# Attention matmuls of both halves together, and both softmax halves first on VectorE, in the first and third cross attention

## What is computed

```python
# A0
Q = q @ Wq.T + bq; K = k @ Wk.T + bk; V = k @ Wv.T + bv
scores = einsum('bhqd,bhkd->bhqk', Q_, K_) / D_HEAD ** 0.5
scores = where(causal, scores, -1e9)
att = einsum('bhqk,bhkd->bhqd', softmax(scores), V_)
att_h = layer_norm(att + q)
# A2
scores = einsum('bqhd,bkhd->bhqk', q, k)
scores = where(mask == 0, -1e20, scores)
out = einsum('bhqk,bkhd->bqhd', softmax(scores / sqrt(EMBED)), v)
x = layernorm(out @ w_out + b_out + query)
```

## Time and profile before

| | us |
|---|---|
| median of three executions | 2589.75 |
| the profiled execution | 2593.18 |
| its span, first to last instruction | 2591.4 |
| A0, first to last score product | 14.9 to 412 |
| A2, first to last score product | 1029 to 1404 |

### The profile page before, as it was taken

One profiled execution on the slowest core, in us unless ns is written; L12 is line 12 of the kernel. 1 busy time (PEld: TensorE's weight loads), 2 busy tenths in 40 slices (PEclk: granted clock), 3 DMA queues, 4 the chain that ended last, 5 costly groups with the idle time before them and its releaser, 6 DMA issues. The chain is left out here.

```text
span 2591.4 us, 83416 instructions
## 1 busy us (share of the span) xinstructions
PE 2355.9 (91%) x26926; PEld 1806.6 (70%) x26926; DVE 1894.2 (73%) x4003; ACT 1498.3 (58%) x3407; POOL 1539.6 (59%) x2438
## 2 busy tenths in 40 slices
PE   6999998987777777999998988999999999999899
PEld 4666666975656565777776876777777777777587
DVE  4676764139999994677776667888888888888566
ACT  4777775558888884777776542444444444444333
POOL 2555555127888884455556776666666666666332
PEclk9999999989999997999999998999999999999999
DMA  4111111235555551222121223333333333333111
GB/s 121 38 38 39 36 40 44 71 109 153 148 155 148 154 153 39 51 46 46 47 47 41 65 63 83 92 94 97 97 95 95 94 94 96 94 94 93 50 58 54
DMA packets 443043, 211.78 MB, mean 82 GB/s; under 512 B 206400, under 2 KB 433856, under 8 KB 442816
## 3 DMA queue, kind: packets, MB, share of 16 engines
q1 hardware_dynamic: 442944, 210.51, 30.7%
HBM read 113.36 MB, written 29.88 MB: 55 GB/s over the span
## 5 line engine op out<-in xcount | busy, mean ns | idle before, releaser
L666 PE MATMUL bank<-sb_ident,sb_region 128*77 128x128 f32 x3072 | 413.8, 278 | 85.7 <-ACT sb_pT L754 84.8
L666 PEld LDWEIGHTS bank<-sb_ident,sb_region 128*77 128x77 f32 x3072 | 350.2, 151 | 139.9 <-issue 137.7
L754 ACT ACTIVATE sb_pT<-bank 77x1024 f32<-77x1024 f32 x384 | 391.6, 1020 | 67.1 <-PE bank L666 67.0
L858 DVE TENSOR_REDUCE sb_max<-bank 128x8 f32<-128x616 f32 x256 | 203.5, 795 | 205.8 <-PE bank L648 118.0
L1528 ACT ACTIVATE sb_l<-sb_l 128x640 f32<-128x640 f32 x128 | 94.5, 738 | 386.2 <-DVE sb_l L1576 386.2
L749 ACT ACTIVATE sb_region<-sb_region 128x616 f32<-128x616 f32 x384 | 276.8, 721 | 1.4 <-POOL sb_region L995 1.4
L1649 POOL TENSOR_TENSOR sb_pn<-sb_l,sb_r_all 128x512 f32<-128x512 f32 x128 | 134.7, 1052 | 233.4 <-DVE sb_r_all L1586 229.5
L1398 PE MATMUL bank<-sb_region,sb_wqkv 128*128 128x128 f32 x2048 | 255.2, 279 | 1.6 <-DVE sb_region L1564 0.8
L682 PE MATMUL bank<-sb_pT,sb_v 77*32 77x128 f32 x6144 | 248.2, 279 | 3.6 <-ACT sb_pT L754 3.2
L1438 PE MATMUL bank<-sb_wvo,sb_region 128*64 128x512 f32 x1024 | 248.0, 605 | 0.0
L1398 PEld LDWEIGHTS bank<-sb_region,sb_wqkv 128*128 128x128 f32 x2048 | 243.6, 195 | 4.1 <-DVE sb_region L1564 1.5
(11 more groups left out here) (183 smaller groups left out, 5645.4 us busy)
## 6 DMA issues: line engine op xcount, KB each, us to landing
sb_region<-in_side SPq DMA_DIRECT2D x64, 616.0 KB, 3.8
sb_pT<-sb_region SPq DMA_DIRECT2D x512, 64.0 KB, 2.1
sb_kF<-sb_region SPq DMA_DIRECT2D x512, 64.0 KB, 2.1
scratch_after_A<-sb_y SPq DMA_DIRECT2D x256, 64.0 KB, 1.8
sb_fx<-scratch_after_A SPq DMA_DIRECT2D x96, 128.0 KB, 2.1
sb_mask<-in_mask SPq DMA_DIRECT2D x64, 154.0 KB, 2.2
sb_x<-scratch_after_F SPq DMA_DIRECT2D x128, 64.0 KB, 1.9
sb_ctx<-in_ctxT SPq DMA_DIRECT2D x192, 38.5 KB, 1.9
```

The lines of the kernel that those rows point to most:

```text
L666: mm = nc.tensor.transpose(two[0:C, h * T:(h + 1) * T], p_s[b.par][:, head * C:(head + 1) * C], ident[:])
L754: nc.scalar.activation(pT_s[k][:], two[0:C, :], ACT.Copy).then_inc(pT_kept.sem(b), 1)
L858: nc.vector.tensor_reduce(dst, by_bank_and_head(scores_half(k)), AX.X, ALU.max).then_inc(max_made.sem(b), 1)
```

## The change

In A0 and A2, TensorE's `attend(b, 0)` is taken from the end of step b and done in step b + 1, straight before `attend(b, 1)`, behind `scores(b + 2)`. On VectorE, `peak` and `shift` of the second half follow those of the first at once; `invert`, `normalise` and `sums` come after both. `sum_context(b+1)` moves to the end of the step, and the statistics are taken at the end of a step (of b - 2) and no longer at the start of the next one (of b - 3), which is the same batch. No operation is added or taken away, and A1 keeps its order.

```diff
--- before.py
+++ after.py
@@ -598,6 +598,7 @@
             w = cross[ph]
             prev = phase_before(ph)
             taken = s_weighted if ph == "A1" else shifted
+            together = ph != "A1"
 
             def out_banks_left(b):
 
@@ -708,6 +709,8 @@
                 if has(1):
                     scores(b + 1)
                 if has(-1):
+                    if together:
+                        attend(b + -1, 0)
                     attend(b + -1, 1)
                 if has(-2) and ph != "A0":
                     transpose_o(b + -2, has(1))
@@ -737,7 +740,7 @@
                     transpose_x(b + 3)
                 if has(2) and ph == "A0":
                     mask_early(b + 2, b + 1 if has(1) else None)
-                if has(0):
+                if has(0) and not together:
                     attend(b, 0)
             drive(pe, NB, step, reach=REACH)
 
@@ -959,26 +962,25 @@
                     aggregate(b + -2)
 
             def step(b, has):
-                if has(1) and ph == "A0":
-                    sum_context(b + 1)
-                if has(-3):
-                    statistics(b + -3)
                 if has(1):
                     peak(b + 1, 0)
                 if has(-3):
                     aggregate(b + -3)
                 if has(1):
                     shift(b + 1, 0)
+                    peak(b + 1, 1)
+                    shift(b + 1, 1)
                 if has(-1):
                     invert(b + -1)
                     normalise(b + -1)
                 if has(-2):
                     sums(b + -2)
-                if has(1):
-                    peak(b + 1, 1)
-                    shift(b + 1, 1)
+                if has(1) and ph == "A0":
+                    sum_context(b + 1)
                 if has(2) and ph == "A2":
                     key_bias(b + 2)
+                if has(-2):
+                    statistics(b + -2)
             drive(dve, NB, step_weighted if ph == "A1" else step, reach=REACH)
 
         def cross_gpsimd(pool, ph):
```

## The result

The changed kernel takes 2629.97 us (median of four executions, 2629.05 to 2633.8) against 2590.8 us before (2586.35 to 2592.21). The ratio is 1.0153, with a 95% interval of 1.0138 to 1.0167: 39 us slower, where 42 had been forecast. The profiled execution took 2630.25 us, its span 2628.5.

A forecast was written before the change was run, and what follows sets the result against it. TensorE's in-order queue, with scores waiting for the query copy, was taken as the bound. Over 64 steps each, A0 +16.6 us and A2 +25.6 us, together 42.2 on 2589.8, gave 2632 us; range 2606 to 2656.

The forecast's parts named there:

- The bound: A0 and A2: TensorE's in-order queue plus small stalls sets the period, TensorE busy 92 to 94%; scores need the query copy.
- The attention block at its new place: Between scores and attention of half 1: paid in full, adding 0.45 us a step (0.33 to 0.58).
- The saving at its old place: End of step: mostly covered by the query copy wait; saves 0.14 us in A0, nothing in A2.
- An ordinary step: Saving and added block summed: +0.31 us in A0, +0.45 us in A2.
- The loop's end: Jump of TensorE's four-step loop, 0.21 us in A0, 0.20 in A2: hidden afterwards, -0.05 us a step.
- The steps written out at the ends of the phases: Steps outside the hardware loop in A0 and A2: counted like the others, within 64 steps a phase.
- the clock: Granted clock in A0 and A1: at its upper level, 1.00, so left out of the sum.
- The spare time of the normalisation: VectorE's delayed normalisation before the query projection: 0.3 us to spare in A0, so no cost.
- rival C: VectorE becomes late: each 0.1 us beyond the spare 0.3 costs 6.4 us a phase; 2645 us, chance 0.10.
- The stall of the keys: Keys wait 0.17 us for VectorE's first shift in A0: goes away, but not on the path.
- rival B: The keys' stall was on the path: A0 gains 0.17 to 0.2 us a step more; 2620 us, chance 0.08.
- Rival A: Mode changes decide, query wait doesn't hold TensorE: -0.13 us a step in A0, -0.24 in A2; 2566 us, chance 0.09.

The follow-up runs named there:

- e7: The changed kernel with the attention of half 0 computed a second time, unused, at its old place at the end of the step: 2639.65 us, ratio 1.0199.
- e3: The kernel before with only TensorE's new order, VectorE keeping its old step: 2630.06 us, ratio 1.0156.
- e5: The kernel before with query projection and transpose of x moved ahead of the transposes of half 1 in A0 and A2: 2556.4 us, ratio 0.9872.
- e4: The changed kernel with TensorE's order put back, so only VectorE's order is new: 2612.0 us, ratio 1.0090.
- e9: e6 with VectorE's order changed to peak 0, shift 0, peak 1, invert, normalise, shift 1, sums: 2532.35 us, ratio 0.9778.
- e6: e5 plus the paired attention and ScalarE's query and x copies ahead of the first exponential, VectorE's order old: 2577.5 us, ratio 0.9949.

## Why the prediction was right, point by point

**The bound.** That TensorE's chain through the query copy sets the period held: filling its shadow (e7) cost nothing in A2 and 0.14 us in an ordinary step of A0, as the release 0.13 earlier lets expect, and VectorE's order didn't change the changed kernel's time (e3). That e5 gained 35 us by moving the copy ahead fits it, but e5 fills a second stall too. Since e3 has the old VectorE order and the same time, the later `sum_context`, and the context load behind it, cost nothing either, as forecast.

**The attention block at its new place**, taken at 0.45, measured 0.43 (1.01 for the pair less 0.58 for one).

**The saving at its old place.** A0: release 0.20 behind the copy's end was taken, 0.19 measured (205.84 to 206.03), so 0.13 was saved for 0.14. A2: nothing, as forecast (0.92 for 0.89).

**An ordinary step**: A0 +0.31 forecast, +0.29 to +0.30 measured; A2 +0.45 and +0.45 (6.32 for 5.87).

**The loop's end** was mis-sized. I counted its 0.21 and 0.20 us as hidden behind the wait for the query copy. It still costs 0.15 in A0 (6.58 for 6.43), and in A2 0.18 (the scores 1.10 behind the transpose of x for 0.92). Of the 0.05 a step that were taken off, 0.035 to 0.045 weren't saved, about 2 us in A0 and 3 in A2 too little in the sum. What in TensorE's queue holds it there wasn't tried.

**The steps written out at the ends of the phases** were counted like the others, and that was too much by more than the first error was too little. A0 from its first to its last score product grew by 13.8 us (397.3 to 411.1) for a forecast of 16.6, A2 by 24.6 (374.8 to 399.5) for 25.6; at the growth of the steps in the loop, 0.28 and 0.43, they would have grown by 17.7 and 27.6. Two things are seen. A written-out step grows less: in A0 from 6.14 to 6.35 (before, 28.14 to 34.28; after, 27.66 to 34.01), since the late mask starts 0.82 behind the transpose of x there and not 0.91, in A2 from 5.87 to 6.14. And the first steps of A0 run into a wait for a context load, before (first row) and after (second row):

```profile
53.30 0.68 PE L620 MATMUL bank<-sb_ctx,sb_L_xattn_wk 128*128 128x77 f32 x2 [4.11 <-DMA sb_ctx<-in_ctxT]
```

```profile
53.08 0.42 PE L621 MATMUL bank<-sb_ctx,sb_L_xattn_wk 128*128 128x77 f32 x2 [3.31 <-DMA sb_ctx<-in_ctxT]
```

Both go on at 53. At the scores before the wait the changed kernel is 0.1 us late (46.70 for 46.56), at the third ones behind it 0.9 early (70.17 for 71.10). A part of this is the clock, which the forecast had left out of the sum. After the idle time of 4.11 and 3.31 us the granted clock is at its lower level, 1.2 GHz, for a while: 0.50 over 53 to 58 us before, and a mean of 0.57 over 54 to 58 in the changed kernel, which had still run at 1.00 from 53 to 54. The rows are as in the earlier trace rows, before and after:

```profile
53.00:58.00 5.00, 4.70 (x33) 3.96 (x33) 0.43 (x2) 2.37 (x6) 1.57 (x3) 0.50 0.29 65
```

```profile
54.00:58.00 4.00, 3.96 (x29) 2.04 (x31) 0.00 (x1) 2.67 (x6) 1.50 (x3) 0.57 0.32 85
```

So the sum is nearer than its terms. The loop's end made it 5 us too small and the ends of the phases 7 too large; that these nearly cancel is luck. The cost of an ordinary step is not.

**VectorE.** The spare time of the normalisation was worked out as 0.3 us in A0 and is 0.3 in the trace, so rival C stayed off. This spare time exists only by the added block, which the 4.86 for 4.41 counted without saying so: e4 shows the same order costing 23 us without it. The stall of the keys went, as forecast, and the step grew by the 0.30 of the sum without rival B, not by the 0.12 with it, so rival B is out. One reading was off without harm: with the block the keys were to be due 2.84 behind the scores, not 3.0 (2.39 and 0.45), and came at 2.79; the first shift ended at 2.50. Rival A has the saving by the pair about right (0.15 of two single blocks, for 0.13) and the time wrong by 64 us. The rule of the Trainium skill that it goes with (TensorEngine Tiling (Array Packing), Key Properties), that changing the tiling mode drains the engine, agrees with this 0.15.

## What to carry to other kernels

Before moving work out of a queue's tail, ask what the next instruction there waits for: work that fills the shadow of another engine's copy is free, and the same work behind it costs its full length (here 0.43 us against nothing in A2 and 0.14 in an ordinary step of A0, where it is longer than the shadow by that much). A reordering can be right and its partner missing: the pair lost 39 us while the query copy was on the chain and was worth 72 us in e9, where the copy was off it and VectorE had the second peak in its idle time. Compare such a kernel with the best one without the change as well: against e5 it was 24 us. After each bottleneck is removed read the waits again, phase by phase: e6 shows the next one at once, in A2 and hardly in A0.

## What the runs showed of the hardware that I had not expected

The jump at the end of TensorE's loop costs 0.15 to 0.18 us even where TensorE idles 0.4 to 0.65 us beside it. In the written-out steps the same instructions start sooner behind the query copy than in the loop: the scores of A2 in the changed kernel 0.73 to 0.74 us behind the transpose of x (1067.76 for 1067.02), for 0.92 in the loop; why wasn't tried. A block of 16 matmuls added to every step (e7) left the granted clock at its upper level, as did the idle time in the changed kernel: 1.00 in both over 120 to 390 and 1070 to 1390 us, as before.
